# Grouped attention with four heads' keys stacked in one tile, and a new order of scores and maxima

## The chip, the cores and the metric

The kernel runs on one core of a Trainium2 chip. The metric is the time of one execution on the device, in microseconds (us), taken as the median of several runs. A profile is one further execution, recorded instruction by instruction. TensorE is called PE, VectorE DVE, ScalarE ACT, GpSimd POOL and SyncE SP, as in the profile.

## What is computed

The reference is a chain of nine blocks on an activation of 4 batches x 512 tokens x 256 features: a Mamba-like scan, a mixture of experts, an attention with rotary factors ("rotary"), the experts again, a plain attention that is later gated ("pattern"), a latent attention, a second mixture of experts, an attention with grouped heads and a memory ("grouped"), and those experts again. The change touches three of them, rotary, pattern and grouped. In outline they compute

```
rotary, pattern: 16 heads of width 16, each with its own keys and values
grouped:         32 query heads of width 8 over 8 key/value heads
for each batch and head h:
    s = softmax(q_h @ k_h.T * scale)      # 512 x 512
    o_h = s @ v_h
out = concat(o_h) @ Wo                    # grouped: mixed with elu(q) @ memory
```

## The kernel before, in words

All data stay in SBUF in transposed form, features on the partitions and the 512 tokens of a batch along the free axis. The stages run one after another; within a stage each engine has its own instruction stream, and all streams are generated from one list of events, written out by hand, so that the order of the events is the order on every engine. An engine that must wait for another blocks everything behind it in its own stream.

The class `Heads` (line 931) is shared by the three stages. It works on groups of four query heads. A batch has `G4` groups (4 in rotary and pattern, 8 in grouped), a stage `NG` groups (16, 16 and 32). For each group the events are these.

- `ek` and `eq` (lines 1077 and 1078): two selection matmuls each bring the parts of the heads' keys and queries into place in a PSUM bank, and ACT copies them to SBUF. A head takes `rows` partitions of a tile: 64 in rotary and pattern (two heads per tile, two tiles per group), 32 in grouped (four heads in one tile). These rows hold the high and the low part of the numbers and one row for a bias.
- `mx` (line 1081): for each head and each of the four blocks of 128 queries a matmul of the queries by all 512 keys, of which DVE takes the negative row maximum (line 1149). That makes 16 maxima per group. They are for the group that comes next: while group g has its scores computed, the maxima of g + 1 are found.
- `bias` (line 1086): four small matmuls turn the maxima round, and DVE adds them to the bias row of the queries (line 1155). After it, the scores come out of the matmul with their maximum already taken away.
- `s` (line 1090): scores of one head and one block of 128 keys, 128 x 512, into one of three score banks. ACT takes the exponential (line 1126). A group has 4 key blocks `kt`, each with four scores, for heads 0 to 3.
- `pv` (line 1096): the exponentials of a key block times the values, four heads side by side in 32 columns each. It runs one key block behind the scores.
- `sums` (ACT, line 1133), `norm` (DVE, lines 1160 to 1171) and `o cut` (POOL, lines 330 and 332): the group's output is copied out, normalised, and split into high and low part for the output projection `out`.

Matmuls other than scores use four auxiliary PSUM banks in turn (`AUXB`), so each of them waits until the result four places earlier has been read. The score of number n waits for the exponential of number n - 3.

`schedule` builds the order. Each group has 12 slots, three per key block: slot 3kt after the first pair of scores, 3kt + 1 after the second pair, 3kt + 2 after the `pv`. Other work of the stage (the next batch's layer norm, its projections `qk` and `v`, the memory, the output projection `out`, in rotary also `rot` and `hv`) is put into slots by the stage functions. The maxima of the next group are put in front of what the slots hold, in these counts:

```python
for pos, count in ((0, 1), (1, 3), (3, 3), (4, 2), (6, 2), (7, 2), (9, 3)):
```

so 4, 5, 4 and 3 maxima fall to the four key blocks, and within a slot pair half of the slot's events stand between the two scores. Slot 4 ends with the `norm` of the group before, slot 10 has the `bias` of the next group (slot 5 too where there are two tiles), slot 11 the stacks of the group after next.

In rotary and pattern the four heads of a group are computed on their own 64 rows: `k_rows` and `q_rows` slice the tiles to the half in which the head lies. In grouped it is different. There each of the 8 key heads has a tile of 128 rows of its own (`k_alone`, `KZ`), which is zero except for 32 rows. The matmul runs over all 128 rows, and the zeros cancel the three other query heads. These tiles are zeroed once by DVE (line 1139), and ACT fills them for each batch with four copies of 32 rows per `ek` event (line 1111), eight copies in all. The stacks of a batch, `ek` among them, stand in slot 11 two groups ahead.

In grouped the first group of a batch also has the next batch's layer norm (lines 296, 313, 324). Two groups of a batch have a projection whose result goes through ACT, DVE and POOL back to ACT (lines 2289, 2357, 2318, 2320, 2292 to 2294), and two groups have the memory matmuls and their DVE work (lines 2360 to 2368).

## Time and profile before

| | |
|---|---|
| median of 3 runs | 4565.31 us (4560.84 to 4579.52) |
| profiled execution | 4568.12 us, of which the span from first to last instruction is 4566.3 us |
| mean granted TensorE clock | 0.912 of full speed |
| PE busy | 3840.6 us (84%) |
| DVE busy | 2580.8 us (57%) |
| ACT busy | 1687.5 us (37%) |
| POOL busy | 1353.1 us (30%) |
| chain that ended last | PE 54%, DVE 22%, ACT 5%, POOL 3% |

Busy time is the time in which at least one instruction of the engine is recorded as running. The chain that ended last starts from the last instruction and goes back at each step to what released it; it tells which work set the end. The three stages of the change take about 1590 of the 4566 us, so the shares of the whole program say little about them. The views have to be read stage by stage: the windows for busy time and clock, the chain of waits in one group for what bounds it, and the timeline for the distance between two matmuls.

### The profile page before, as it was taken

The page shows a single profiled execution, that of the slowest core. Times are in us where ns is not written, and L with a number is a line of the kernel's source. Part 1 is how long each engine was busy: PE and PEld are TensorE (multiplying, and loading weights), DVE is VectorE, ACT ScalarE, POOL GpSimd, SP SyncE. Part 2 cuts the span into 40 slices and gives each one's busy share as a digit, 9 for nine tenths or more (in the row PEclk, how much of TensorE's full clock was granted, in tenths as well). Part 3 has the DMA queues.
Part 4 walks back from the last instruction along what each step waited for, and adds up shares of the span by engine and source line. Part 5 has one row for each costly group of instructions (what it writes and reads, how often), then busy time and mean ns, then how long its engine had stood idle before and what let it go on. Part 6 is the DMA issues. An engine that isn't in the chain of part 4 may idle for free.

```text
span 4566.3 us, 44420 instructions
## 1 busy us (share of the span) xinstructions
PE 3840.6 (84%) x15840; PEld 2548.4 (56%) x15840; DVE 2580.8 (57%) x4324; ACT 1687.5 (37%) x2807; POOL 1353.1 (30%) x1074
## 2 busy tenths in 40 slices
PE   6869778887978883888889887999878888879999
PEld 4647544435844432555555555788744444457887
DVE  5645366654456652678686765433356766655333
ACT  2433256653235540232323223222245555522222
POOL 3234322214320102333323314444322221143442
PEclk8989889988989976999999998999989999979999
DMA  1010000001000002101000101000000000010000
GB/s 56 1 37 5 29 1 1 1 1 41 1 22 5 5 5 80 28 16 26 18 24 17 26 16 58 18 27 9 16 1 1 1 1 1 1 58 21 25 13 19
DMA packets 32760, 83.27 MB, mean 18 GB/s; under 512 B 6304, under 2 KB 7456, under 8 KB 32288
## 3 DMA queue, kind: packets, MB, share of 16 engines
q1 hardware_dynamic: 32544, 80.44, 5.7%
q8 instruction: 130, 2.13, 0.2%
q14 instruction: 86, 0.70, 0.0%
HBM read 59.44 MB, written 4.19 MB: 14 GB/s over the span
## 4 chain that ended last, share of the span: by engine, by line
PE 54%; DVE 22%; ACT 5%; POOL 3%; issue 2%; DMA 1%; SPq 1%; DVEq 0%; POOLq 0%; ACTq 0%
PE ps L226 11%; PE ps L227 10%; PE ps L228 10%; DVE max_cols L1149 7%; PE ps L1096 5%; PE ps L1935 3%; PE ps L1090 2%; PE ps L296 2%; DVE q_lo L2112 2%; DVE max_cols L2128 2%; PE ps L1081 2%; ACT probs L1126 1%; PE ps L1086 1%; PE ps L800 1%; PE ps L1077 1%
## 5 line engine op out<-in xcount | busy, mean ns | idle before, releaser
L1149 DVE TENSOR_REDUCE max_cols<-ps 128x1 fp32r<-128x512 f32 x1024 | 635.6, 680 | 284.9 <-PE ps L1081 284.1
L1126 ACT ACTIVATE probs<-ps 128x512 f32<-128x512 f32 x1024 | 546.1, 603 | 256.5 <-PE ps L1090 164.6
L754 POOL TENSOR_TENSOR h_lo<-h,h_hi 128x512 fp32r<-128x512 f32 x304 | 392.5, 1291 | 816.6 <-ACT h_hi L834 816.6
L911 DVE TENSOR_TENSOR gated<-silu,ps 128x512 f32<-128x512 f32 x288 | 197.9, 687 | 689.1 <-PE ps L228 665.7
L828 ACT ACTIVATE silu<-ps 128x512 f32<-128x512 f32 x304 | 181.9, 598 | 928.0 <-PE ps L228 927.9
L226 PE MATMUL ps<-xn_hi,w_hi 128*128 128x512 f32 x1216 | 479.5, 394 | 0.0
L227 PE MATMUL ps<-xn_lo,w_hi 128*128 128x512 f32 x1216 | 476.0, 391 | 0.0
L228 PE MATMUL ps<-xn_hi,w_lo 128*128 128x512 f32 x1216 | 475.8, 391 | 0.0
L1096 PE MATMUL ps<-probs,v_aug 128*32 128x512 f32 x2048 | 310.3, 683 | 0.0
L330 POOL CAST o_hi<-o_scaled 128x512 fp32r<-128x512 f32 x64 | 39.1, 612 | 910.1 <-DVE o_scaled L1171 910.1
L1935 PE MATMUL ps<-probs,v_tok 128*128 128x512 f32 x512 | 263.5, 611 | 2.7 <-ACT denominators L1997 2.7
L226 PEld LDWEIGHTS ps<-xn_hi,w_hi 128*128 128x128 f32 x1216 | 231.0, 190 | 49.8 <-issue 1.0
L227 PEld LDWEIGHTS ps<-xn_lo,w_hi 128*128 128x128 f32 x1216 | 230.4, 189 | 49.6 <-issue 1.4
L228 PEld LDWEIGHTS ps<-xn_hi,w_lo 128*128 128x128 f32 x1216 | 230.0, 189 | 48.6
L226 PE MATMUL ps<-h_hi,w_hi 128*128 128x512 f32 x608 | 249.4, 410 | 1.2 <-POOL h_lo L754 1.2
L1090 PE MATMUL ps<-q_stack,k_alone 128*128 128x512 f32 x512 | 213.9, 440 | 31.3 <-ACT probs L1126 29.1
L227 PE MATMUL ps<-h_lo,w_hi 128*128 128x512 f32 x608 | 239.7, 394 | 0.0
L228 PE MATMUL ps<-h_hi,w_lo 128*128 128x512 f32 x608 | 239.6, 394 | 0.0
L1090 PE MATMUL ps<-q_stack,k_stack 64*128 64x512 f32 x512 | 198.8, 485 | 43.3 <-ACT probs L1126 41.2
L1987 ACT ACTIVATE probs<-ps 128x1024 f32<-128x1024 f32 x128 | 131.2, 1025 | 279.1 <-PE ps L1932 278.9
L1081 PE MATMUL ps<-k_alone,q_stack 128*128 128x512 f32 x512 | 201.7, 432 | 37.8 <-ACT q_stack L1115 23.7
L2128 DVE TENSOR_REDUCE max_cols<-ps 128x1 fp32r<-128x512 f32 x256 | 169.2, 682 | 89.6 <-PE ps L1921 89.3
(460 smaller groups left out, 7896.1 us busy)
## 6 DMA issues: line engine op xcount, KB each, us to landing
raw<-in_w_ffn SPq DMA_DIRECT2D x76, 448.0 KB, 3.3
raw<-raw SPq DMA_DIRECT2D x256, 64.0 KB, 2.0
composed_inputs<-in_m_latent SPq DMA_DIRECT2D x1, 5120.0 KB, 15.5
raw<-in_w_mamba SPq DMA_DIRECT2D x8, 448.0 KB, 5.9
raw<-in_w_latent SPq DMA_DIRECT2D x5, 448.0 KB, 16.8
x<-in_x SPq DMA_DIRECT2D x4, 512.0 KB, 6.2
gated_pattern<-gated SPq DMA_DIRECT2D x4, 512.0 KB, 3.1
raw<-gated_pattern SPq DMA_DIRECT2D x4, 512.0 KB, 4.3
```

Source lines behind the costliest of these rows:

```text
L226: nc.tensor.matmul(psum, wh, xh, start=start, stop=False)
L227: nc.tensor.matmul(psum, wh, xl, start=False, stop=False)
L228: return nc.tensor.matmul(psum, wl, xh, start=False, stop=stop)
L754: nc.gpsimd.tensor_tensor(HL[:, b % 3, :], hb[:, b % 2, :], HH[:, b % 3, :].bitcast(F32), ALU.subtract).then_inc(G.sem, G.step((s, ev)))
L911: nc.vector.tensor_tensor(ga if routed(i) else hb[:, i % 2, :], sg[:, i % 2, :], bank[2 + i % 2], ALU.mult).then_inc(V.sem, V.step((s, "ga ...
L1081: last = nc.tensor.matmul(self.psum(ev), self.q_rows(g, h)[:, q * P:(q + 1) * P], self.k_rows(g, h), start=True, stop=True)
L1090: last = nc.tensor.matmul(self.scores(self.step_no(g, kt, h)), self.k_rows(g, h)[:, kt * P:(kt + 1) * P], self.q_rows(g, h), start=True, s ...
L1096: last = nc.tensor.matmul(bank[6][32 * h:32 * h + 32, :], self.VA[:, (g // self.G4) % 2, kt, self.khead((g % self.G4) * 4 + h), :], self.P ...
L1126: nc.scalar.activation(self.PB[:, n % 8, :], self.scores(n), ACT.Exp, scale=self.scale).then_inc(A.sem, A.step((s, ("exp", n))))
L1149: nc.vector.tensor_reduce(self.MB[:, self.tile_of(g, h) % 2, q, col:col + 1], self.psum(ev), op=ALU.max, axis=AX.X, negate=True).then_inc( ...
L1935: last = nc.tensor.matmul(bank[6 + i], VT[:, (g // HP) % 2, kt, 64 - 64 * i:192 - 64 * i], PB[:, (g * QT + kt) % 2, i, :], start=kt == 0, ...
L2128: nc.vector.tensor_reduce(MB[:, q, 32 * i:32 * i + 1], bank[slot(ev)], op=ALU.max, axis=AX.X, negate=True).then_inc(V.sem, V.step((s, ev)))
```

## The change

In grouped the eight tiles of 128 rows are given up. The keys are now kept as `k_stack`, two tiles per batch with four key heads each, each head in its 32 rows, as the `ek` matmuls produce them. ACT copies a whole tile at once, the zeroing by DVE is gone, and scores and maxima are computed on 32 rows (`rows_of`). In all three stages the order is new. The maxima of a group are put into the first and second half of each key block by `FIRST_MX`: 2 and 2 in the first key block, 6 and 2 in the second, 2 and 2 in the third, none in the fourth. Within them the heads go in the order 2, 3, 0, 1 in grouped and 1, 0 in rotary and pattern. In grouped a first half is two scores and then maxima, a second half maxima and then two scores. In rotary and pattern the maxima stand between the two scores. The slots' other events follow behind each half in one piece.

```diff
+        FIRST_MX = (0, 2, 4, 10, 12, 14, 16, 16, 16)
-                self.KS = None if k_tiles else alloc("k_stack", [P, 2, self.tiles, L], F32R)
-                self.KZ = alloc("k_alone", [P, 2, self.nkv, L], F32R) if k_tiles else None
+                self.KS = alloc("k_stack", [P, 2, k_tiles or self.tiles, L], F32R)
             def maxima(self, g):
-                return [("mx", g, t * self.per + i, q) for t in range(self.tiles) for q in range(QT) for i in range(self.per)]
+                turn = (2, 3, 0, 1) if self.k_tiles else (1, 0)
+                return [("mx", g, t * self.per + i, q) for t in range(self.tiles) for q in range(QT) for i in turn]
+            def rows_of(self, h):
+                return slice(h % self.per * self.rows, (h % self.per + 1) * self.rows)
             def k_rows(self, g, h):
                 if self.k_tiles:
-                    return self.KZ[:, (g // self.G4) % 2, self.khead((g % self.G4) * 4 + h), :]
+                    return self.KS[self.rows_of(h), (g // self.G4) % 2, self.k_tile_no(g, h), :]
             def q_rows(self, g, h):
-                return self.QS[:, g % 2, h // self.per, :] if self.k_tiles else self.QS[r, g % 2, h // self.per, :]
+                return self.QS[self.rows_of(h), g % 2, h // self.per, :]
             def schedule(self, begin, end, reader):
-                        mx, had = self.maxima(n), 0
-                        for pos, count in ((0, 1), (1, 3), (3, 3), (4, 2), (6, 2), (7, 2), (9, 3)):
-                            self.slots[g][pos] = mx[had:had + count] + self.slots[g][pos]
-                            had += count
-                    for h in range(4):
-                        if n < len(units):
-                            events.append(("s",) + units[n] + (h,))
-                        here = at[h // 2]
-                        events += here[len(here) // 2:] if h % 2 else here[:len(here) // 2]
+                    for k in range(2) if n < len(units) else ():
+                        g, kt = units[n]
+                        one, two = (("s", g, kt, h) for h in (2 * k, 2 * k + 1))
+                        mx = self.maxima(g + 1)[FIRST_MX[2 * kt + k]:FIRST_MX[2 * kt + k + 1]] if g + 1 < self.NG else []
+                        if self.k_tiles:
+                            events += mx + [one, two] + at[k] if k else [one, two] + mx + at[k]
+                        else:
+                            events += [one] + mx + [two] + at[k]
             def act(self, act, s, ev):
-                    for i in range(self.per if self.k_tiles else 1):
-                        r = slice(i * self.rows, (i + 1) * self.rows) if self.k_tiles else slice(0, P)
-                        to = self.KZ[r, (g // self.G4) % 2, t * self.per + i, :] if self.k_tiles else self.KS[:, g % 2, t, :]
-                        nc.scalar.activation(to, self.psum(ev)[r, :], ACT.Identity, bias=self.one[r, :]).then_inc(A.sem, A.step((s, ev)))
+                    to = self.KS[:, (g // self.G4) % 2, t, :] if self.k_tiles else self.KS[:, g % 2, t, :]
+                    nc.scalar.activation(to, self.psum(ev), ACT.Identity, bias=self.one).then_inc(A.sem, A.step((s, ev)))
             def vec_begin(self, dve, s):
-                if self.k_tiles:
-                    nc.vector.memset(self.KZ[:, :, :, :].bitcast(F32), 0.0).then_inc(V.sem, V.step((s, "alone")))
```

## Rows read from the trace of the kernel before

**Rows 1.** Windows: stretch, length, busy us (xinstructions) per engine, granted clock; rotary, pattern, grouped
```profile
530.00:1012.00 482.00, 389.42 (x1648) 191.18 (x1648) 296.08 (x497) 263.06 (x463) 112.60 (x103) 0.87 0.01 2
1290.00:1705.00 415.00, 347.37 (x1596) 174.26 (x1596) 248.90 (x418) 210.08 (x388) 42.17 (x39) 0.87 0.01 4
3300.00:3992.00 692.00, 564.58 (x2544) 291.16 (x2544) 454.72 (x757) 370.41 (x676) 142.45 (x126) 0.92 0.01 2
```

**Rows 2.** Chain that ended last, its shares by line, grouped, 3342 to 3990
```profile
by line: DVE max_cols L1149 26.1%; PE ps L1096 14.4%; PE ps L1081 9.3%; PE ps L1090 8.8%; PE ps L1086 3.0%; ACT k_alone L1111 2.5%; DVE o_turned L1160 2.5%; DVE o_scaled L1171 2.4%; ACT q_stack L1115 2.1%; PE ps L1077 2.0%; issue 1.9%; PE p
```

**Rows 3.** Groups by form, 3342 to 3990: busy us, mean ns, idle before
```profile
L1149 DVE TENSOR_REDUCE max_cols<-ps 128x1 fp32r<-128x512 f32 x512 | 316.7, 679 | 142.9 <-PE ps L1081 142.6
...
L1086 PE MATMUL ps<-h_grouped_hi,max_cols 128*128 128x128 f32 x128 | 22.0, 296 | 32.5 <-DVE max_cols L1149 32.4
...
L1111 ACT ACTIVATE k_alone<-ps,c 32x512 fp32r<-32x512 f32 x24 | 16.3, 680 | 7.3 <-PE ps L1078 6.8
```

**Rows 4.** Windows of single groups of grouped, from one bias to the next
```profile
3499.40:3524.30 24.90, 17.69 (x76) 8.59 (x75) 14.93 (x25) 15.24 (x26) 3.17 (x3) 0.93 0.00 0
...
3563.70:3579.50 15.80, 14.08 (x70) 7.01 (x71) 12.38 (x21) 9.65 (x18) 1.90 (x2) 1.00 0.00 1
3579.50:3601.90 22.40, 17.14 (x76) 8.68 (x76) 13.18 (x22) 11.52 (x22) 8.68 (x7) 0.92 0.00 1
...
3889.40:3906.50 17.10, 15.60 (x71) 7.50 (x71) 12.38 (x21) 9.66 (x18) 1.89 (x2) 0.90 0.00 1
```

**Rows 5.** Chain of a quiet group of grouped: start, us, what; idle rows left out
```profile
3873.56 0.66 PE ps L1086 x4
...
3876.56 0.50 PE ps L1081
...
3879.91 3.09 DVE max_cols L1149 x5
...
3885.16 4.17 DVE max_cols L1149 x7
```

**Rows 6.** Timeline, PE, grouped: first and last of eight matmuls that follow each other
```profile
3899.51 0.50 PE L1090 MATMUL ps<-q_stack,k_alone 128*128 128x512 f32 x1
...
3901.23 0.39 PE L1081 MATMUL ps<-k_alone,q_stack 128*128 128x512 f32 x1
```

**Rows 7.** Timeline, PE, pattern: a selection matmul before scores; then seven matmuls on halves
```profile
1618.83 0.39 PE L1078 MATMUL ps<-heads_lo,h_pattern_hi 128*128 128x512 f32 x1
...
1619.14 0.51 PE L1090 MATMUL ps<-q_stack,k_stack 64*128 64x512 f32 x2
...
1622.29 0.50 PE L1090 MATMUL ps<-q_stack,k_stack 64*128 64x512 f32 x2
...
1622.62 0.63 PE L1081 MATMUL ps<-k_stack,q_stack 64*128 64x512 f32 x4
...
1623.09 0.39 PE L1090 MATMUL ps<-q_stack,k_stack 64*128 64x512 f32 x1
```

**Rows 8.** Chain, group before a new batch: one of eight copies, first matmul after them
```profile
3501.15 0.68 ACT k_alone L1111
...
3507.44 0.50 PE ps L1081
```

**Rows 9.** Chain, group with the projection through POOL: score behind it, and the values
```profile
3593.26 0.80 PE ps L1090
3594.06 1.87 PE ps L1096 x8
```

**Rows 10.** Timeline, start of grouped: zeroing, the layer norm's matmuls and DVE step, eight copies
```profile
3303.21 6.88 DVE L1139 MEMSET k_alone<- 128x8192 f32 x1 [1.66 <-issue]
...
3306.30 3.72 PE L296 MATMUL ps<-x,c 128*128 128x512 f32 x4 [11.40 <-POOL spare L222]
...
3310.65 1.27 DVE L313 TENSOR_TENSOR xc<-x,ps 128x512 f32<-128x512 f32 x2
...
3335.71 5.62 ACT L1111 ACTIVATE k_alone<-ps,c 32x512 fp32r<-32x512 f32 x8 [1.03 <-PE ps L1078]
```

More of the change, by code:

```diff
@@ L973, in maxima @@
             def maxima(self, g):
-                return [("mx", g, t * self.per + i, q) for t in range(self.tiles) for q in range(QT) for i in range(self.per)]
+                turn = (2, 3, 0, 1) if self.k_tiles else (1, 0)
+                return [("mx", g, t * self.per + i, q) for t in range(self.tiles) for q in range(QT) for i in turn]
+            def rows_of(self, h):
+                return slice(h % self.per * self.rows, (h % self.per + 1) * self.rows)
             def k_rows(self, g, h):
-                r = slice((h % self.per) * self.rows, (h % self.per + 1) * self.rows)
                 if self.k_tiles:
-                    return self.KZ[:, (g // self.G4) % 2, self.khead((g % self.G4) * 4 + h), :]
-                return self.KS[r, g % 2, h // self.per, :]
+                    return self.KS[self.rows_of(h), (g // self.G4) % 2, self.k_tile_no(g, h), :]
+                return self.KS[self.rows_of(h), g % 2, h // self.per, :]
             def q_rows(self, g, h):
-                r = slice((h % self.per) * self.rows, (h % self.per + 1) * self.rows)
-                return self.QS[:, g % 2, h // self.per, :] if self.k_tiles else self.QS[r, g % 2, h // self.per, :]
+                return self.QS[self.rows_of(h), g % 2, h // self.per, :]
             def k_tile_no(self, g, h):
@@ L1105, in act @@
                     act.wait_ge(PE.sem, PE.at((s, ev)))
-                    if self.k_tiles and g == 0:
-                        act.wait_ge(V.sem, V.at((s, "alone")))
-                    for i in range(self.per if self.k_tiles else 1):
-                        r = slice(i * self.rows, (i + 1) * self.rows) if self.k_tiles else slice(0, P)
-                        to = self.KZ[r, (g // self.G4) % 2, t * self.per + i, :] if self.k_tiles else self.KS[:, g % 2, t, :]
-                        nc.scalar.activation(to, self.psum(ev)[r, :], ACT.Identity, bias=self.one[r, :]).then_inc(A.sem, A.step((s, ev)))
+                    to = self.KS[:, (g // self.G4) % 2, t, :] if self.k_tiles else self.KS[:, g % 2, t, :]
+                    nc.scalar.activation(to, self.psum(ev), ACT.Identity, bias=self.one).then_inc(A.sem, A.step((s, ev)))
                 elif kind == "eq":
```

## Prediction

> **What bounds the kernel now.** The change touches three stages, so I first read the windows of those stages [rows 1]. Rotary, pattern and grouped take 482, 415 and 692 us. In none of them is an engine full: in grouped PE is busy for 565 us, DVE for 455 and ACT for 370. Nobody is the bound alone, so the time must be set by a chain that passes from engine to engine. The second view is therefore the chain by line in grouped [rows 2]. Over those 648 us the row maxima on DVE hold 26.1%, the matmuls of maxima and scores 9.3% and 8.8%, and the copies into the zero-padded key tiles 2.5%. So the two matmul lines hold 18.1% of 648, that is 117 us, and the copies 16 us. These are the parts that the change shortens.
>
> The third view is one quiet group, a group with no other stage work [rows 4, 5]. It takes 15.8 us from bias to bias. The bias starts at 3873.56 and the first matmul of the next maxima at 3876.56, 3.0 us later, behind the values, the stack and its copy. From there 3.35 us pass until DVE begins a run of five maxima, 3.09 us. The normalisation stands between 3883.00 and 3885.16, 2.16 us, and seven more maxima take 4.17 us. The next bias follows at once. DVE is what ends this group. Sixteen maxima take 16 x 0.60 = 9.7 us, and with the normalisation DVE needs 11.9 us after the first result. The reader is to see that DVE pays for only two gaps: the 3.0 us around the bias, and about 1 us between the fourth and the fifth maximum, where PE is late.
>
> **The padded matmuls.** In grouped eight matmuls of scores and maxima on 128 rows start from 3899.51 to 3901.23, 1.72 / 7 = 0.24 us apart [rows 6]. In pattern, where two neighbours lie on different halves, seven start from 1622.29 to 1623.09, 0.80 / 6 = 0.13 us apart, and the four recorded together as L1081 x4 take 0.63 us [rows 7]. So two matmuls on different rows run side by side. The trace shows no matmul of 32 rows. Its price lies between 0.24 (nothing overlaps) and a quarter of that, 0.06 (four overlap). I take 0.13, the nearest row. For 512 + 512 matmuls that is 0.11 x 1024 = 113 us of PE time. Only what is on the chain counts, and there DVE is close behind, as the quiet group shows.
>
> The Trainium skill (TensorE: Matmul & The Clock Gate, "Part 3: Packing small matmuls") gives a packing of four 32-row matmuls as 3.07 times as fast. By that a matmul would cost 0.24 / 3.07 = 0.08, an estimate from that page, and my sum would change by at most 0.05 us in each run of six matmuls on the chain, some 5 us over the stage. The trace has no such matmul and can't confirm it.
>
> A change of the array's shape costs something: a 64-row score begins 0.31 us after the full-row selection matmul ahead of it, not 0.24 [rows 7]. In grouped such changes are added between the stack and the scores, before the bias and around other work, about 4 per group: 4 x 0.07 x 32 = 9 us of PE time, a third of it on the chain, 3 us. The Trainium skill (TensorEngine Tiling (Array Packing), "Key Properties") states that changing the tiling mode drains TensorE; it speaks against this change, and the 0.31 agrees in sign.
>
> **The sum for grouped, by kinds of group.**
> - Start: eight copies of 32 rows took 5.62 us [rows 10]. Two whole-tile copies at about 0.7 (a copy's time hardly depends on its rows: 0.68 for 32) take 1.4, all on the path to the first maxima: -4.2. The zeroing ran from 3303.21 to 3310.09 and DVE's next step was at 3310.65 [rows 10]. The layer norm's matmuls ended at 3306.30 + 3.72 = 3310.02, so only the 0.6 goes; the rest of the 6.9 us was hidden by them. Together -4.8.
> - Group before a new batch, three of them, 24.9 us [rows 4]: eight copies of 0.68 with their gaps, 5.6 us, stand on the chain ahead of the query copy and the first matmul [rows 8]. Two remain: -4.2 each. Behind it, from 3507.44 to the bias at 3524.3 are 16.9 us; DVE needs 0.5 + 9.7 + 2.16 + 2.55 (memory work; DVE busy 14.93 against 12.38 [rows 4]) = 14.9, if it is never short of maxima: -2.0. Together 3 x 6.2 = -18.6.
> - Quiet groups, 17 of 32 (three in each of the first three batches, all of the last): with four maxima issued ahead of the next `pv` and the fifth to twelfth right behind it, PE is back within 2.2 us of the first result while DVE has 2.4 us to do. The gap closes: 3.0 + 0.5 + 9.7 + 2.16 = 15.3 instead of 15.8 [rows 4, 5], 17 x 0.5 = -8.5.
> - Two groups per batch, six in all, 22.4 us, where ACT waits for POOL and the exponentials queue behind it [rows 4, 9]. PE reaches that point 0.5 us earlier. From the released score at 3593.26 to the bias at 3601.90 were 8.6 us: 0.8, values 1.87 [rows 9], eight matmuls with a slow start 2.35, values 1.0, and the rest, 2.6, the last maxima. After the change DVE has done its 12 maxima during the wait; there remain 0.8 + 1.87 + 1.3 + 1.0 and four scores behind their exponentials, 1.1, so 6.1. That is -2.5 (I leave the 0.5 as reserve), -15.
> - Memory group -1.3 and layer-norm group -0.3, three each: in these the eight maxima of the second key block come ahead of work that PE or DVE is late with anyway. -5.
> - Shape changes +3.
>
> -4.8 - 18.6 - 8.5 - 15 - 5 + 3 = -49.
>
> **The clock.** A quiet group at a granted clock of 0.90 takes 17.1 us, at 1.00 15.8 [rows 4]. After the change PE has less to do and waits longer, both in the second key block and ahead of the bias. Pattern, where matmuls already run in pairs, has 0.87 over its stage against 0.92 in grouped [rows 1]. I charge 1.3 us to six more groups: +8. Bounds: 0, and 1.3 x 32 = +42.
>
> **The order in all three stages.** The second key block now has 8 maxima where it had 5. With four auxiliary banks PE can be only four ahead of DVE, so scores two to four and the `pv` wait about 3 x 0.6 = 1.8 us longer. Queued behind them are the exponentials of ACT and whatever stands in slots 3 to 5, and behind the longer row of maxima on DVE the normalisation, so POOL's split of the output and then `out`. In exchange the fourth key block has none. Before, it had three maxima and the bias waited for the last; in grouped PE stood 32.5 us before L1086 [rows 3]. A run of scores there was bound by three maxima, about 0.8 + 0.5 + 1.9 = 3.2 us, and now by the exponential that the fourth score waits for, 1.1: about 2 us come back. So for a group whose chain is PE's it is even, and for one whose chain is DVE's it plays no part. In rotary and pattern a few neighbours on the same half become alternate, some six per group at 0.11 us, a quarter of that on the chain: 32 x 0.17 = -5. Bounds for the two stages: -20 (the bias wait goes entirely) and +25 (0.8 us not returned in each of 31 groups). SP isn't touched: no DMA is added, removed or passed.
>
> **Sum.** -49 + 8 - 5 = -46. Against the profiled execution of 4568.1 (span 4566.3 and 1.8 around it) that is 4522. The median of the runs is 2.8 below the profiled one, which gives 4519; with rounding of the reserve above I forecast 4518.
>
> **The rivals.**
> 1. Forecast: the parts above, between -25 and -75: 4490 to 4540. For it: each part is a gap in a chain of this trace. Chance 0.50.
> 2. DVE becomes the bound everywhere. Then grouped costs DVE's 455 us of work [rows 1], 32 x 3.5 = 112 around the biases, and about 28 in which DVE is idle before the first maxima: 595 of 692, so -97. Against it: layer norm, POOL and ACT waits stay in a third of the groups. Between -75 and -110: 4458 to 4490, point 4475. Chance 0.16.
> 3. The change doesn't do what it says: 32-row matmuls don't overlap, or DVE has no use for them earlier. Then the copies remain, -4.8 - 12.6 = -17, with the clock against it: between 0 and -23, 4542 to 4565, point 4551. For it: 142.9 us of DVE's idle time ended with L1081 [rows 3], but much of that is the stack's chain and not the rate of matmuls. Chance 0.21.
> 4. Slower: the second key block. Its 1.8 us are paid in all 63 groups that have a successor, 113 us, and the fourth block returns only the measured wait, 32.5 / 31 = 1.05 each, 66 us; less the copies 17 and pairs 10 the kernel is 20 us slower, 4588. It decides where less than 1.8 - 27 / 63 = 1.4 us comes back. For it: scores are fed late, and ACT had waited for PE before. Against it: ACT is busy for 9.65 of 15.8 us in a quiet group and can catch up [rows 4]. Between 0 and +45. Chance 0.13.
>
> **How the numbers follow.** The likeliest is the forecast, 4518. The range for 8 in 10 reaches over it and rival 2 down to 4460, and over rival 3 up to 4562; it leaves out a tail of rival 2 and nearly all of rival 4, some 0.16. Half a per cent, about what a measurement of this kernel can tell from no change, is 23 us. Faster by more than that: forecast and rival 2, 0.66. Within it: rival 3 and 0.02 of rival 4, 0.23. Slower: the rest of rival 4, 0.11.
>
> **What would show it.** Right: in grouped, scores and maxima 0.13 us apart or closer, two L1111 copies per batch, no zeroing, the DVE runs of maxima up to the normalisation 12 long, the group before a new batch near 19 us, the quiet one near 15.3. Wrong: 0.24 between 32-row neighbours (rival 3); a quiet group above 16 with PE waiting for L1149 ahead of a score in the second key block and ACT idle behind it (rival 4); a granted clock in grouped well under 0.90 (the clock's charge too small); rotary or pattern changed by more than 20 us.

## The result, and the profile after

| | before | after |
|---|---|---|
| median | 4568.98 us (4560.84 to 4579.52) | 4643.25 us (4632.99 to 4655.24) |
| ratio | | 1.0168 [1.0143, 1.0193] |
| profiled execution | 4568.12 us, span 4566.3 | 4632.99 us, span 4631.2 |
| mean granted clock | 0.912 | 0.874 |

The change makes the kernel 1.7% slower. Forecast was a gain of 46 us. Measured is a loss of 74 between the medians of four runs each, and of 65 between the profiled executions. On the page of the kernel after, PE holds 60% of the chain, where it held 54%, and DVE 16%, where it held 22%. The clock row, in 40 slices of 115.8 us, shows the place: the slices in which grouped lies, from 3348 to 4053 us, are the thirtieth to the thirty-fifth, and they stand at 7, 7, 6, 7, 7 and 5 tenths.

```profile
span 4631.2 us, 44387 instructions
...
PEclk8989888888978986999999989999877677579999
...
PE 60%; DVE 16%; ACT 5%; POOL 3%; issue 2%; DMA 1%; SPq 1%; POOLq 0%; DVEq 0%; ACTq 0%
```

From here on a stage's length runs from its first maxima matmul to its last `pv`. The windows of rotary, pattern and grouped in the kernel after (stretch, length, busy time and instructions of PE, PEld, DVE, ACT and POOL, granted clock, DMA share, GB/s):

```profile
601.70:1041.10 439.40, 384.80 (x1593) 184.12 (x1596) 271.45 (x456) 254.24 (x441) 86.22 (x78) 0.86 0.00 1
1333.90:1713.60 379.70, 338.78 (x1526) 165.83 (x1530) 237.69 (x400) 200.72 (x372) 38.62 (x36) 0.88 0.01 5
3348.40:4053.50 705.10, 621.72 (x2492) 239.20 (x2494) 437.18 (x738) 337.62 (x635) 126.62 (x112) 0.69 0.00 1
```

The grouped stage of the kernel before, same view:

```profile
3342.00:3989.10 647.10, 546.68 (x2494) 281.07 (x2494) 438.76 (x738) 356.52 (x653) 126.75 (x111) 0.94 0.00 1
```

Rotary took 422.1 us before and 439.4 after, pattern 384.3 and 379.7, grouped 647.1 and 705.1. Grouped alone is 58 us longer, with nearly the same number of PE instructions, 18 copies of ACT fewer, and a clock of 0.69 in place of 0.94. The rest of the difference is rotary's 17.3, less 5.1 at the start of grouped and 4.6 in pattern.

### The profile page after: what moved, and what is told of

It reads as the page before. It is cut to its first block, busy times and chain, and to the rows that moved or that the text cites. A ratio compares the mean times of both kernels' runs of the same rounds, so it can differ in the third digit from the quotient of the medians.

```text
span 4631.2 us, 44387 instructions
## 1 busy us (share of the span) xinstructions
PE 3945.4 (85%) x15840; PEld 2519.1 (54%) x15840; DVE 2570.0 (55%) x4323; ACT 1668.9 (36%) x2783; POOL 1352.7 (29%) x1074
## 4 chain that ended last, share of the span: by engine, by line
PE 60%; DVE 16%; ACT 5%; POOL 3%; issue 2%; DMA 1%; SPq 1%; POOLq 0%; DVEq 0%; ACTq 0%
PE ps L226 10%; PE ps L228 10%; PE ps L227 10%; PE ps L1098 7%; PE ps L1092 4%; DVE max_cols L1145 3%; PE ps L1083 3%; PE ps L1931 3%; PE ps L296 2%; DVE max_cols L2124 2%; ACT probs L1124 2%; DVE q_lo L2108 2%; PE ps L1088 1%; PE ps L1079 1%; PE ps L800 1%
## 5 line engine op out<-in xcount | busy, mean ns | idle before, releaser
L1145 DVE TENSOR_REDUCE max_cols<-ps 128x1 fp32r<-128x512 f32 x1024 | 627.7, 680 | 226.1 <-PE ps L1083 216.5
L1092 PE MATMUL ps<-q_stack,k_stack 64*128 64x512 f32 (+1 forms) x1024 | 393.8, 566 | 77.1 <-ACT probs L1124 76.8
L1083 PE MATMUL ps<-k_stack,q_stack 64*128 64x512 f32 (+1 forms) x1024 | 373.0, 524 | 99.7 <-DVE q_stack L1151 26.6
L1098 PE MATMUL ps<-probs,v_aug 128*32 128x512 f32 x2048 | 370.9, 806 | 0.0
L1092 PEld LDWEIGHTS ps<-q_stack,k_stack 64*128 64x128 f32 (+1 forms) x1024 | 160.5, 217 | 330.9 <-ACT probs L1124 189.2
L1083 PEld LDWEIGHTS ps<-k_stack,q_stack 64*128 64x128 f32 (+1 forms) x1024 | 160.6, 209 | 245.3 <-issue 117.0
## 6 DMA issues: line engine op xcount, KB each, us to landing
raw<-in_w_latent SPq DMA_DIRECT2D x5, 448.0 KB, 16.8
```

Of the source, the lines that this page charges most:

```text
L1083: last = nc.tensor.matmul(self.psum(ev), self.q_rows(g, h)[:, q * P:(q + 1) * P], self.k_rows(g, h), start=True, stop=True)
L1092: last = nc.tensor.matmul(self.scores(self.step_no(g, kt, h)), self.k_rows(g, h)[:, kt * P:(kt + 1) * P], self.q_rows(g, h), start=True, s ...
L1098: last = nc.tensor.matmul(bank[6][32 * h:32 * h + 32, :], self.VA[:, (g // self.G4) % 2, kt, self.khead((g % self.G4) * 4 + h), :], self.P ...
L1145: nc.vector.tensor_reduce(self.MB[:, self.tile_of(g, h) % 2, q, col:col + 1], self.psum(ev), op=ALU.max, axis=AX.X, negate=True).then_inc( ...
```

## Did the matmuls overlap?

Yes, and more than I assumed. The timeline of PE in the kernel after (start, us, engine, line, operation):

```profile
3900.05 0.39 PE L1080 MATMUL ps<-heads_lo,h_grouped_hi 128*128 128x512 f32 x1
3900.37 0.50 PE L1092 MATMUL ps<-q_stack,k_stack 32*128 32x512 f32 x2
3901.13 0.72 PE L1083 MATMUL ps<-k_stack,q_stack 32*128 32x512 f32 x4 [0.26 <-ACT q_stack L1113]
```

Four maxima matmuls together take 0.72 us, where one alone takes about 0.5: so on average they end some 0.07 apart ((0.72 - 0.50) / 3). DVE gets its long run, twelve maxima in 7.28 us, in the chain of waits: the first line below, from the group that begins at 3898.12. The other lines of that view are from a quiet group at half clock, 3935.59 to 3956.09:

```profile
3901.66 7.28 DVE max_cols L1145 x12
...
3935.66 1.04 PE ps L1088 x4
...
3941.92 1.86 PE ps L1098 x8
...
3945.45 2.56 PE ps L1083 x4
...
3948.04 1.86 PE ps L1098 x8
...
3952.10 1.86 PE ps L1098 x8
...
3956.16 1.04 PE ps L1088 x4
```

Of DVE's sixteen maxima only one, of 0.69 us, is left on this chain. Every `pv` is on it, with 1.86 us for eight matmuls, and the bias takes 1.04 where it took 0.66 [rows 5]. The bias windows of two neighbouring quiet groups, with the same instructions in both:

```profile
3918.79:3935.59 16.80, 14.81 (x72) 5.22 (x71) 12.29 (x21) 9.69 (x20) 1.88 (x2) 0.78 0.01 2
3935.59:3956.09 20.50, 19.05 (x72) 6.43 (x71) 12.39 (x21) 9.68 (x19) 1.88 (x2) 0.50 0.00 1
```

DVE and ACT do the same work in both. PE is busy 4.2 us longer in the second and the group is 3.7 longer. Its clock is 0.50, the lower of the two levels, 1.2 GHz. So the stage went from a chain that DVE closes to a chain of PE at a slower clock. The groups by form in grouped show the same over the whole stage. First the kernel after (columns as in [rows 3]), then the kernel before:

```profile
L1145 DVE TENSOR_REDUCE max_cols<-ps 128x1 fp32r<-128x512 f32 x512 | 313.2, 681 | 121.8 <-PE ps L1083 121.8
...
L1098 PE MATMUL ps<-probs,v_aug 128*32 128x512 f32 x1024 | 205.8, 890 | 0.0
...
L1088 PE MATMUL ps<-h_grouped_hi,max_cols 128*128 128x128 f32 x128 | 30.6, 380 | 1.5 <-DVE max_cols L1145 1.5
```

```profile
L1096 PE MATMUL ps<-probs,v_aug 128*32 128x512 f32 x1024 | 147.8, 652 | 0.0
```

DVE idled 142.9 us before its maxima and now idles 121.8. The wait of the bias for them went from 32.5 [rows 3] to 1.5. Both went the way of the forecast. But the values, which the change does not touch, cost 205.8 us in place of 147.8. On the chain by line the maxima on DVE fall from 26.1% of 648 [rows 2] to 6.7% of 706, that is by 122 us, while `pv` rises from 14.4% [rows 2] to 26.0% (+90) and the scores from 8.8% to 15.4% (+52):

```profile
by line: PE ps L1098 26.0%; PE ps L1092 15.4%; PE ps L1083 11.1%; DVE max_cols L1145 6.7%; ACT probs L1124 6.0%; PE ps L1088 4.0%; PE ps L2261 3.0%; PE ps L1079 2.7%; PE ps L296 2.3%; issue 2.3%; ACT q_stack L1113 1.8%; PE ps L1080 1.6%; PO
```

What was open is why the clock falls: the order, the idle time of PE, the short matmuls, or the rows.

## Experiments

All lengths are those of the profiled executions. In e4, e7 and e12 the results of the added matmuls are overwritten. A granted clock between 0.50 and 1.00 is the mean of a stretch with parts at either level.

| | rotary, clock | pattern, clock | grouped, clock | ratio to before |
|---|---|---|---|---|
| before | 422.1, .89 | 384.3, .88 | 647.1, .94 | 1 |
| after | 439.4, .86 | 379.7, .88 | 705.1, .69 | 1.0168 [1.0143, 1.0193] |
| e1_rows | 418.1, .90 | 368.8, .93 | 722.4, .69 | 1.0167 [1.0149, 1.0185] |
| e2_order | 437.3, .87 | 385.1, .86 | 645.1, .95 | 1.0054 [1.0027, 1.0081] |
| e3_grouped_only | 422.6, .89 | 375.5, .91 | 709.0, .69 | 1.0116 [1.0086, 1.0147] |
| e4_filler | 447.3, .84 | 382.4, .88 | 1093.0, .66 | 1.1017 [1.0985, 1.1049] |
| e5_half_columns | 424.2, .89 | 371.6, .92 | 642.6, .89 | 0.9996 [0.9981, 1.0011] |
| e6_spread | 418.8, .90 | 387.1, .87 | 682.4, .91 | 1.0095 [1.0063, 1.0128] |
| e7_scores_twice | 425.4, .90 | 384.1, .87 | 764.3, .71 | 1.0282 [1.0236, 1.0329] |
| e8_head_by_head | 435.1, .87 | 375.5, .90 | 727.9, .70 | 1.0212 [1.0165, 1.0258] |
| e9_half_rows | 422.5, .89 | 368.7, .93 | 713.8, .79 | 1.0131 [1.0111, 1.0152] |
| e10_full_rows | 437.4, .94 | 393.5, .96 | 652.2, .93 | 1.0083 [1.0066, 1.0100] |
| e11_early_keys | 411.5, .92 | 376.8, .90 | 639.8, .93 | 0.9969 [0.9958, 0.9979] |

A stage whose code is the same scatters: pattern with the old order reads 368.7 to 384.3 in six kernels (before, e1, e3, e5, e9, e11), rotary 411.5 to 424.2. Less than some 15 us in one stage of one execution is no finding.

### e1_rows and e2_order: the two halves of the change

e1 keeps the 32-row tiles and takes the order of before:

```diff
-                turn = (2, 3, 0, 1) if self.k_tiles else (1, 0)
-                return [... for i in turn]
+                return [... for i in range(self.per)]
```

with the table of slots and the loop over `h` of before. e2 is before with `FIRST_MX`, `turn` and the new loop, and its 128-row tiles.

> The changed kernel with the order of before in all three stages; what is left of the change is the 32-row tiles and the two whole-tile copies in grouped. Theory A (the clock falls because matmuls on 32 rows that run side by side leave TensorE too little to do): grouped, from its first L1081/L1083-type maximum to its last pv, stays long, 675 to 710 us against 647 before and 705 after, granted clock there under 0.80; rotary 422 as before. Theory B (the clock falls because the run of eight maxima makes TensorE wait): clock there 0.90 or more, grouped 590 to 625 us, kernel about 30 us faster than before.

> The kernel of before with the new order alone; in grouped the 128-row zero-padded tiles and the eight copies stay. Theory A: clock in grouped 0.88 or more, grouped 635 to 655 us against 647 before; kernel +10 to +20 us, from rotary. Theory B: clock in grouped under 0.80, grouped 690 us or more.

Measured: the windows of grouped, e1 first, then grouped and rotary of e2.

```profile
3320.40:4042.80 722.40, 603.67 (x2494) 238.81 (x2494) 438.25 (x738) 339.58 (x635) 126.52 (x112) 0.69 0.00 1
```

```profile
3356.00:4001.10 645.10, 561.64 (x2494) 277.44 (x2494) 436.88 (x738) 353.67 (x653) 126.61 (x111) 0.95 0.00 1
...
601.20:1038.50 437.30, 379.42 (x1594) 180.54 (x1596) 271.21 (x456) 253.72 (x441) 86.10 (x78) 0.87 0.00 1
```

The rows alone carry the whole loss in grouped: 0.69 appears with them and not with the order. Theory A of e1 had the clock right; the stage, 722.4 us, is longer than its 675 to 710. The order alone leaves grouped where it was, and makes rotary 15 us longer. The eight runs of e2 lie apart, four from 4565.85 to 4577.37 us and four from 4598.84 to 4607.01. The stages shown are of one of the lower ones, 4575.35; where the upper ones lose some 29 us more is not known. On 32 rows the new order reads 17 us less (705.1 against 722.4), hardly more than the scatter.

### e3_grouped_only: the order of before in rotary and pattern

```diff
-                turn = (2, 3, 0, 1) if self.k_tiles else (1, 0)
+                turn = (2, 3, 0, 1) if self.k_tiles else (0, 1)
```

and the old table and loop where `not self.k_tiles`.

> The changed kernel with the order of before in rotary and pattern only. If the new order is what lengthened rotary (422 to 439 us from first maximum to last pv) and left pattern (384 to 380), rotary returns to 422 and pattern to 384, grouped stays at about 705, and the kernel is 10 to 15 us faster than after. If rotary's 17 us were scatter between executions, nothing moves by more than 5.

Rotary is back at 422.6, grouped stays at 709.0. The kernel's median is 25 us under that of the one after. 10 to 15 were expected; rotary accounts for 17, the rest is within what stages of the same code scatter.

### e4_filler: a full-row matmul ahead of every score

```diff
+                    if self.k_tiles:
+                        nc.tensor.matmul(self.scores(...), self.SEL["ident"], self.QS[:, g % 2, 0, :], start=True, stop=True)
```

> The changed kernel with one more matmul in grouped: ahead of each score a full 128-row matmul of 512 columns into the same bank, whose result the score overwrites; 512 matmuls, 123 us of TensorE time at 0.24 each. Theory A (the clock follows the work that TensorE is given): clock in grouped back to 0.90 or more and grouped 580 to 650 us, shorter than after although work is added. Theory B (the waits behind DVE set the clock) or a loss that isn't the clock's: grouped 705 us or longer, up to 820.

Both theories failed: the stage took 1093 us at 0.66. Its window, then a stretch of the timeline of its PE and the clock there, show why.

```profile
3352.90:4445.90 1093.00, 1062.74 (x3006) 415.19 (x3006) 441.92 (x738) 375.31 (x635) 126.26 (x112) 0.66 0.00 1
```

```profile
3510.37 0.50 PE L1094 MATMUL ps<-q_stack,k_stack 32*128 32x512 f32 x1
3510.80 0.50 PE L1093 MATMUL ps<-q_stack,h_grouped_hi 128*128 128x512 f32 x1
3511.22 0.50 PE L1094 MATMUL ps<-q_stack,k_stack 32*128 32x512 f32 x1
```

```profile
3511.00:3513.00 2.00, 2.00 (x9) 0.85 (x8) 1.21 (x2) 1.25 (x3) 0.00 (x0) 1.00 0.00 0
```

A 32-row matmul and a 128-row one in turn begin 0.43 us apart, each way and at a clock of 1.00, where neighbours of one shape are 0.24 apart [rows 6]. The 512 fillers bring two changes of shape each. PE is busy for 97% of the stage, and yet it gets through 3006 matmuls in 1093 us, 2.75 per us, where the kernel after has 3.5. So the filler did not make PE's work denser, it made it thinner, and this run can't tell the rows from the other causes. It does price the change of shape.

### e7_scores_twice and e8_head_by_head: more of the same rows, and no overlap

```diff
-                    last = nc.tensor.matmul(self.scores(...), ...)
+                    for _ in range(2 if self.k_tiles else 1):
+                        last = nc.tensor.matmul(self.scores(...), ...)
```

> The changed kernel with each 32-row score matmul of grouped issued twice into the same bank, so 512 more matmuls but no more changes of shape. They lie on the same rows, so they can't run side by side: about 0.24 us more for each, 123 us. Theory A: the clock in grouped rises from 0.69 to 0.80 or more, and the stage takes 690 to 740 us against 705. Rival (low clock of the 32-row form whatever the work): clock 0.70 or less, stage above 760.

```diff
+                if self.k_tiles:
+                    return [("mx", g, h, q) for h in (2, 3, 0, 1) for q in range(QT)]
```

> The changed kernel with the maxima of grouped in the order head by head, four query blocks on the same 32 rows in a row, so that most maxima can't run side by side. Theory A (less busy TensorE): the maxima take 0.24 us each again, TensorE is busier, clock in grouped 0.75 or more. Theory C (few rows at work): clock 0.69 or less although nothing overlaps, stage 705 to 740 us.

Grouped in e7, then in e8:

```profile
3338.80:4103.10 764.30, 691.34 (x3005) 287.49 (x3006) 439.18 (x738) 348.14 (x635) 126.54 (x112) 0.71 0.00 1
```

```profile
3339.90:4067.80 727.90, 654.65 (x2490) 272.78 (x2494) 437.24 (x738) 340.43 (x635) 126.51 (x112) 0.70 0.00 1
```

PE is busy for 90% of the stage, as against 84% in before (546.7 of 647.1), and the clock is still 0.71 and 0.70. In both runs theory A failed. The times are those of e7's rival and of e8's theory C; the clocks are a hundredth above what these allowed. So it isn't the share of time in which PE is busy. Nor is it that matmuls lie beside each other: with four neighbours on one quarter the clock is the same, and the stage only loses the overlap, 23 us.

### e9_half_rows: 64 rows

Before, with its padded tiles read in the half where the head lies:

```diff
-                    return self.KZ[:, (g // self.G4) % 2, ..., :]
+                    return self.KZ[self.half(h), (g // self.G4) % 2, ..., :]
+            def half(self, h):
+                return slice(h // 2 * 64, h // 2 * 64 + 64)
```

and `q_rows` likewise.

> The kernel of before; in grouped scores and maxima run over the 64-row half of the padded tile in which the head's 32 rows lie. Order, tiles and copies stay. Theory R (the clock follows how many of the array's rows are at work per time): the clock in grouped lies between 0.69 (32 rows) and 0.94 (128 rows), about 0.82, and the stage between 647 and 722 us, about 670. Theory C (only the 32-row form is bad): clock 0.92 or more, stage 640 or less.

```profile
3333.60:4047.40 713.80, 590.71 (x2494) 255.02 (x2494) 438.00 (x738) 354.23 (x653) 126.14 (x111) 0.79 0.00 1
```

Everything but the rows is before's: order, copies, zeroing. 128 rows give 0.94, 64 rows 0.79, 32 rows 0.69. The rows left out hold nothing but zeros in the key tile. Theory R's bounds held; its point, 670 us, was 44 short: 64 rows already cost 67 us, where 32 rows in the same order and with fewer copies cost 75 (e1).

Fewer rows in scores and maxima also bring changes of shape, since `pv`, bias and selection stay on 128 rows. The stages of e1 and e9 change both together. e7, with 512 more small matmuls and not one change of shape more, speaks against the changes as the cause of the low clock, and e12 has none within its streams.

### e12_streams: the rows by themselves

```diff
+                for rows, turn, count in ((128, 1, 96), (64, 2, 192), (128, 1, 96), (32, 4, 384), (128, 1, 96), (32, 1, 96), (128, 1, 96)):
+                    for n in range(count):
+                        r = slice(n % turn * rows, (n % turn + 1) * rows)
+                        nc.tensor.matmul(to[n % turn], ident[r, :], q[r, :], start=True, stop=True)
```

put ahead of the first score of grouped, 1056 matmuls that wait for nobody. It ran once.

> A measurement of the clock by itself: before, with matmuls of 512 columns without any wait ahead of the first score of grouped, whose results are overwritten: 96 on 128 rows, 192 on 64 rows in two halves in turn, 96 on 128 rows, 384 on 32 rows in four quarters in turn, 96 on 128 rows, 96 on the same 32 rows, 96 on 128 rows; each run takes 20 us or more. Theory R (rows at work): clock 1.0 in the 128-row runs and where halves or quarters run side by side (0.12 and 0.06 to 0.11 us each), and 0.5 within the run on the same 32 rows (0.43 us each). Theory U (any unbroken stream holds the clock): 1.0 in all, 0.24 us each in the last.

Windows of these matmuls alone (stretch, length, PE busy, PEld busy, clock, DMA share, GB/s). They are, in order: 128 rows, two halves in turn, four quarters in turn, the start of the same quarter over and over, its continuation twice, and 128 rows again.

```profile
3360.00:3365.00 5.00, 5.00 (x24) 4.00 (x23) 1.00 0.00 0
...
3380.00:3385.00 5.00, 5.00 (x46) 4.32 (x44) 1.00 0.00 0
...
3425.00:3430.00 5.00, 5.00 (x92) 4.17 (x88) 1.00 0.00 0
...
3465.00:3470.00 5.00, 5.00 (x21) 3.89 (x20) 0.88 0.00 0
3470.00:3475.00 5.00, 5.00 (x14) 3.80 (x13) 0.50 0.00 0
...
3495.00:3500.00 5.00, 5.00 (x13) 3.85 (x12) 0.50 0.00 0
...
3510.00:3515.00 5.00, 5.00 (x23) 4.01 (x22) 1.00 0.00 0
```

PE is busy 5.00 of 5.00 us in each. A window counts every matmul that touches it, so the counts are a little high: from first to last start the 384 on quarters in turn lie 0.058 us apart on average, those on 128 rows 0.23, and those on one quarter 0.43 once the clock has fallen. With all rows at work, whether by one matmul or by two or four beside each other, the clock is 1.00, the level of 2.4 GHz. With one quarter at work it falls to 0.50, 1.2 GHz, stays there, and is back at 1.00 with the 128 rows behind. Theory R held in each stretch. So in these streams the clock goes with how much of the array is at work, and by e9 rows of zeros count as at work.

The Trainium skill (TensorE: Matmul & The Clock Gate, "Part 1: The HAM clock gate") says that the clock depends on how busy PE has been. That agrees with these rows only if busy is meant of the array's rows: by the profile's busy time the fourth to sixth stretches are as full as the first. The Trainium skill (the same page, "Part 3: Packing small matmuls") gives a measured speedup of 3.07 for four quarters. Here they start 0.058 us apart against 0.23, 4 times, as long as nothing stands between them.

### e5_half_columns: fewer columns, all rows

Before, with half the columns in the maxima matmuls of grouped, and DVE reading these twice so that its work stays (its line is left out here):

```diff
+                    n = L // 2 if self.k_tiles else L
-                    last = nc.tensor.matmul(self.psum(ev), ..., self.k_rows(g, h), ...)
+                    last = nc.tensor.matmul(self.psum(ev)[:, 0:n], ..., self.k_rows(g, h)[:, 0:n], ...)
```

> The kernel of before (128-row padded tiles, its order); in grouped each maxima matmul streams 256 keys instead of 512, and DVE reads these 256 results twice, so that its work stays the same. The maximum is taken over half the keys only; the softmax is mathematically the same. TensorE has 512 x 0.11 = 56 us less to do, and no shape changes. Theory A (the clock follows the work that TensorE is given, whatever its shape): clock in grouped falls from 0.94 to 0.85 or less, and the stage takes 640 us or more against 647. Theory C (the clock falls because of the 32-row form or its overlap, not because of less work): clock 0.92 or more, stage 610 to 635 us.

```profile
3335.90:3978.50 642.60, 519.41 (x2494) 271.44 (x2494) 437.52 (x738) 352.79 (x653) 126.38 (x111) 0.89 0.00 1
```

The half of 512 matmuls of 0.22 us is 56 us of PE work. The stage is 4.5 us shorter, less than its scatter, and the whole kernel measures no change. The clock fell by 0.05, PE's busy time by 27 us only. Work taken off PE here is paid back, by the slower clock and in waits: 27 us of the 56 are gone from the busy time, and its idle time grew from 100 to 123. How much of either is the clock's this run doesn't say. The clock, 0.89, lies between what the two theories asked for; the time is theory A's. In the runs with all rows and columns and no even spread (before, e2, e10, e11) grouped reads 0.93 to 0.95, so the clock also falls where no shape and no number of rows changes.

### e6_spread and e10_full_rows: what about rotary?

e6 is e2 with the maxima spread evenly, two to each pair of scores:

```diff
-        FIRST_MX = (0, 2, 4, 10, 12, 14, 16, 16, 16)
+        FIRST_MX = (0, 2, 4, 6, 8, 10, 12, 14, 16)
```

> The kernel of before with the new alternation of scores and maxima, but two maxima to each half of each key block (4, 4, 4, 4 instead of 4, 8, 4, 0). Theory: the eight maxima in the second key block are what lengthened rotary to 437 to 439 us. Then rotary is 415 to 425 here. Rival: the alternation or the split of the slots' events did; then it stays at 435 or more. Grouped 635 to 655 either way.

Rotary, then grouped:

```profile
604.20:1023.00 418.80, 352.38 (x1597) 170.95 (x1596) 272.73 (x456) 251.73 (x441) 85.99 (x78) 0.90 0.00 1
...
3336.40:4018.80 682.40, 560.11 (x2491) 289.05 (x2494) 438.49 (x738) 356.13 (x653) 126.44 (x111) 0.91 0.00 1
```

In rotary the burst of eight maxima is what costs: 418.8 spread, 437.3 in a burst. The five kernels with the burst there (after, e2, e4, e7, e8) read 425.4 to 447.3, mean 436.9, the six with the old order 411.5 to 424.2, mean 420.2. In grouped the spread is 37 us worse than the burst, which I had not expected (635 to 655). The bias line by form in grouped, e6 and then e2, shows the place:

```profile
L1087 PE MATMUL ps<-h_grouped_hi,max_cols 128*128 128x128 f32 x128 | 23.0, 306 | 51.5 <-DVE max_cols L1150 51.5
```

```profile
L1087 PE MATMUL ps<-h_grouped_hi,max_cols 128*128 128x128 f32 x128 | 19.3, 274 | 4.3 <-DVE max_cols L1150 4.3
```

In e6 the fourth key block has four maxima, and only two scores stand between the last of them and the bias. PE waits 51.5 us there for DVE, against 4.3 with the burst and 32.5 in before [rows 3].

e10 turns the finding round: padded 128-row tiles in rotary and pattern as well.

```diff
-                return self.KS[r, g % 2, h // self.per, :]
+                return self.KZ[:, g % 2, h, :]
```

with the copies head by head and the zeroing that belong to it.

> The opposite step: before, but in rotary and pattern too each head's keys get a zero-padded tile of 128 rows (one copy of 64 rows more on ACT per key tile), so that scores and maxima run over all rows, 0.24 us apart instead of 0.13. Theory R: clock in rotary and pattern rises from 0.89 and 0.88 (0.90 and 0.93, 0.89 and 0.91 in other runs of the same code) to 0.95 or more. The time is open: 32 x 0.11 = 3.5 us per group more matmul work and 1.4 us more of ACT against faster everything else; if the clock is worth more, rotary is under 415 and pattern under 365 us. Theory without rows: clock as before, both stages 10 to 30 us longer.

```profile
604.90:1042.30 437.40, 374.29 (x1597) 199.62 (x1596) 274.44 (x456) 277.28 (x473) 86.05 (x78) 0.94 0.00 1
...
1338.00:1731.50 393.50, 331.08 (x1526) 183.91 (x1530) 239.23 (x399) 226.05 (x403) 38.61 (x36) 0.96 0.01 5
```

The clock rises, from 0.89 and 0.88 (0.89 to 0.92 and 0.88 to 0.93 in the six kernels with the same code) to 0.94 and 0.96. Expected was 0.95 or more. And yet both stages are longer, by 15 and 9 us. At 64 rows padding does not pay here. How much of that is the lost overlap and how much the copies was not separated: ACT is busy 27 and 26 us longer than in the stages of before, PE only 10 and 2.

### e11_early_keys: the copies without the rows

Before, with each batch's `ek` put one by one into earlier groups:

```diff
-                if self.k_tiles and g % self.G4 == 0:
+                if self.k_tiles and g == 0:
+                    if self.k_tiles and g % self.G4 in (2, 5) and g // self.G4 + 1 < NB:
+                        self.slots[g][8].append(("ek", (g // self.G4 + 1) * self.G4, (g % self.G4 - 2) // 3))
```

> Before, with 128-row tiles and its order, but in grouped the two ek events of the next batch stand in slot 8 of the batch's third and sixth group, not both in slot 11 of the seventh ahead of the query copy. The eight ACT copies of 5.6 us then lie in groups in which DVE is the end and ACT has slack. My reading of the copies as 5.6 us on the chain, three times: grouped 647 falls to about 630 and the kernel is 12 to 17 us faster than before. Rival (the copies only move): within 5 us of before.

A group that took copies over, and the group before a new batch:

```profile
3543.74:3562.20 18.46, 16.04 (x72) 8.17 (x73) 12.39 (x21) 11.09 (x21) 1.91 (x2) 0.91 0.00 0
...
3649.77:3668.09 18.32, 15.82 (x74) 7.80 (x74) 14.75 (x25) 9.69 (x19) 3.17 (x3) 1.00 0.00 1
```

The group before a new batch went from 25.5 us to 18.3. But each `ek` now has its copies on both sides of a bias, so four groups took them over: the first two grew by 2.6 and 0.9 us, from 15.8 and 22.4, the other two by 1.3 and 2.0, from 16.5 and 22.9. That is 6.9 us given back of 7.2. The eight groups of this batch together, before and then e11:

```profile
3524.29:3688.25 163.96, 136.57 (x638) 70.98 (x638) 111.59 (x188) 92.71 (x170) 34.75 (x30) 0.96 0.00 1
```

```profile
3504.30:3668.09 163.79, 140.01 (x638) 73.06 (x638) 111.86 (x188) 92.62 (x170) 34.69 (x30) 0.94 0.00 1
```

So within the stage the rival held: the copies only move. Grouped reads 7 us shorter (expected 630, measured 639.8), but 2.7 of these lie in its last seven groups, where nothing was moved. The kernel runs at 0.9969 [0.9958, 0.9979] of before, 15 us between the medians, the only one that beats it. That lies within the expected 12 to 17, but the stage does not show the mechanism behind it, so the hit is luck as far as these traces go, and where the kernel gains is open.

## Why the prediction was wrong

**The clock: the step that failed.** I charged 1.3 us to six groups, +8, with +42 as bound. I thought of the clock as following PE's pauses, and priced it from a group at 0.90. In the kernel after PE pauses less, busy for 88% of the stage (621.7 of 705.1) against 84%, and yet the clock there is 0.69 against 0.94: it fell with the rows (e1, e9, e12). The trace of before had a warning, which I used too weakly: pattern, on 64-row halves, had 0.87 against 0.92 [rows 1]. What the lower clock costs is read from two pairs of like groups. Before: 17.1 us at 0.90 against 15.8 at 1.00 [rows 4], 13 us per unit of clock. After: 20.50 at 0.50 against 16.80 at 0.78, 13 again. Over 32 groups and a fall from 0.94 to 0.69 that is 13 x 0.25 x 32 = 104 us (an estimate, since it assumes that every group reacts as a quiet one). e9 bears the slope out: with order and copies of before and a clock 0.15 lower it gives 13 x 0.15 x 32 = 62 us, and 66.7 were measured, changes of shape included. With the other terms of my sum but the start, -44, it gives 104 - 44 = +60 for the stage, and +58 are measured. That they meet so closely is luck in part, since several of those terms did not come out as priced (below). The size of the charge failed, and with it its bound: +42, against an estimate of 104.

**The padded matmuls.** Right in mechanism, and the price too high: I took 0.13, the quarters cost about 0.07 in the stage and 0.058 in the stream. Had I taken that, the forecast would have been more wrong.

**Changes of shape.** Sized at 0.07 us each. Measured is 0.32 for selection to score (3900.05 to 3900.37), near the 0.31 I used, but 0.43 where the shapes alternate (e4), 0.19 above neighbours of one shape. For four per group that is 4 x 0.08 x 32 = 10 us of PE time by the first and 4 x 0.19 x 32 = 24 by the second, as against my 9. The Trainium skill (TensorEngine Tiling (Array Packing), "Key Properties") says that a change of the tiling mode drains TensorE; 0.43 against 0.24 agrees with it in sign. How the +58 divides between clock and changes of shape is not settled: at a slow clock both are slower.

**Start.** -4.8 predicted. From the memset of the maxima to the first matmul were 43.5 us and are 38.4: -5.1. Right.

**Group before a new batch.** -6.2 each predicted. Between the same two biases of both kernels it was 25.5 and is 22.05, -3.4:

```profile
3521.19:3543.24 22.05, 20.10 (x79) 7.60 (x79) 14.75 (x25) 10.32 (x21) 3.16 (x3) 0.75 0.00 0
```

ACT's work is 5 us less, as foreseen (15.24 in [rows 4]), but the clock is 0.75, not 0.93.

**Quiet groups.** 15.3 predicted. The one shown at 0.78 takes 16.8, one at 0.68 18.7. DVE's gap between the fourth and the fifth maximum closed (twelve in 7.28 us in the group at 3898), and PE is late in its place.

**Groups that wait for POOL.** -2.5 predicted. 22.4 [rows 4] became 25.8, +3.4. The mean clock of this group is 0.57:

```profile
3604.57:3630.35 25.78, 21.90 (x77) 8.12 (x76) 13.10 (x22) 11.73 (x23) 8.64 (x7) 0.57 0.00 1
```

**Order in rotary and pattern.** -5 predicted between -20 and +25. Rotary +17, pattern -5 within its scatter. Here rival 4 was right about the place, the burst of eight maxima in the second key block, and e6 shows it: spread out, the loss is gone. That its 1.8 us are paid and less comes back held for rotary. In grouped it did not hold: the order alone gives 645.1 against 647.1. Nor did the gain that I set against it come: in e2 the wait of the bias fell from 32.5 us to 4.3, and the stage hardly changed.

**The rivals.** Rival 2 (DVE the bound everywhere) fell, its maxima hold 6.7% of the chain. Rival 3 (no overlap) fell with the timeline. Rival 4 gave the right sign, but its mechanism accounts for 17 of the 65 us, and the measured loss is beyond its +45. The case that happened, the clock falling by a quarter, was in the list of what would show the prediction wrong and not among the rivals. It should have been one: "a granted clock in grouped well under 0.90" had a price of up to +42 in my text. With +42 in place of +8 the sum is 4552, still a gain and still in the range: a clock as low as 0.69, or stretches at 0.50, had no price at all.

## What to carry to other kernels

Before cutting the rows of a matmul that is on a PE-bound chain, price the clock for the whole stage: read two like groups at different clocks, and let every matmul of the stage pay, also those that aren't changed. In this kernel 96 rows of zeros cost less than slicing them away (e1, e9), while padding 64-row halves cost more than it gave (e10). Quarters ran four times as fast only in an unbroken stream over all four (e12). Where copies are moved out of the group in which they stand on the chain, count what the groups that take them over lose: here 6.9 of 7.2 us (e11).

## What the chip showed that I had not expected

- An unbroken stream on one quarter of the rows, PE busy 100% of the time, is granted 0.50; the same instructions over four quarters are granted 1.00 and start 0.058 us apart against 0.43.
- In a mixed stage the clock is graded by rows: 0.94 on 128, 0.79 on 64, 0.69 on 32, and rows of zeros count as at work. Changes of shape came with the fewer rows.
- A 32-row and a 128-row matmul in turn begin 0.43 us apart at full clock, against 0.24 for two of 128 rows.
- Taking 56 us of columns from PE (e5) gave 4.5 us back.

Open: the exact split of the 58 us between clock and changes of shape, where the kernel of e11 gains its 15 us, and whether 32-row tiles would gain if something else held the clock. The last needs filler work of the same shape on the other quarters and was not tried.
